# All block turns of the attention weights on VectorE, and one row-maximum instruction over two accumulators

## Time and profile before

| | us |
|---|---|
| median of 3 runs | 1153.29 (1152.88 to 1154.09) |
| the profiled execution, its own time | 1152.18 |
| its span, first to last instruction | 1150.4 |
| PE / DVE / ACT / POOL busy | 1120.2 / 904.9 / 588.6 / 658.0 |
| granted TensorE clock | 1.0 throughout |

### The profile page before, as it was taken

One profiled execution on the slowest core, in us unless ns is written; L12 is line 12 of the kernel. 1 busy time (PEld: TensorE's weight loads), 2 busy tenths in 40 slices (PEclk: granted clock), 3 DMA queues, 4 the chain that ended last, 5 costly groups with the idle time before them and its releaser, 6 DMA issues.

```text
span 1150.4 us, 19136 instructions
## 1 busy us (share of the span) xinstructions
PE 1120.2 (97%) x5885; PEld 856.2 (74%) x5885; DVE 904.9 (79%) x1656; ACT 588.6 (51%) x1332; POOL 658.0 (57%) x476
## 2 busy tenths in 40 slices
PE   7999999999999999999999999999999999999998
PEld 6888888888888888886666767767667666767655
DVE  7998787878787866578597797786887876976977
ACT  7634443434444344447455555555556545565543
POOL 2645252525252524329759579389398498496694
DMA  5441414141414132343324323324225233242241
GB/s 202 147 138 46 138 46 128 55 128 55 128 55 128 55 91 92 129 129 74 91 56 129 88 51 117 91 55 130 71 58 161 55 91 111 55 122 59 55 128 38
DMA packets 76606, 108.44 MB, mean 94 GB/s; under 512 B 7712, under 2 KB 40224, under 8 KB 76576
## 3 DMA queue, kind: packets, MB, share of 16 engines
q1 hardware_dynamic: 76576, 108.07, 31.0%
HBM read 58.76 MB, written 16.78 MB: 66 GB/s over the span
## 4 chain that ended last, share of the span: by engine, by line
PE 68%; POOL 13%; DVE 8%; issue 6%; ACT 4%; DVEq 0%; DMA 0%; POOLq 0%; ACTq 0%; SPq 0%
PE ps_f L992 23%; PE ps_s L992 8%; PE ps_o L2274 7%; PE ps_h L992 7%; POOL spare L1587 6%; PE ps_r L2200 6%; POOL spare L1593 5%; PE ps_r L2233 5%; PE ps_s L2251 4%; PE ps_r L2209 3%; DVE nmax L1860 3%; PE ps_s L2259 2%; DVE z_tmp L1879 2%; ACT probs_odd L1670 1%; POOL z L1605 1%
## 5 line engine op out<-in xcount | busy, mean ns | idle before, releaser
L1860 DVE TENSOR_REDUCE nmax<-ps_s 128x1 f32<-128x512 f32 x256 | 158.5, 680 | 79.0 <-PE ps_s L2251 78.0
L1587 POOL TENSOR_TENSOR spare<-xv,pick 128x512 f32<-128x512 f32 x160 | 184.8, 1155 | 35.0 <-DVE pick L1975 22.1
L1605 POOL TENSOR_TENSOR z<-z,z_tmp 128x1280 f32<-128x1280 f32 x35 | 102.6, 2932 | 138.6 <-DVE z_tmp L1879 136.3
L1593 POOL TENSOR_TENSOR spare<-spare 128x512 f32<-128x512 f32 x128 | 165.6, 1294 | 10.0
L1670 ACT ACTIVATE tmp<-ps_s,nmax 128x512 f32<-128x512 f32 x124 | 85.2, 687 | 97.1 <-DVE nmax L1860 97.1
L2274 PE MATMUL ps_o<-pt,spare 128*64 128x512 f32 x496 | 113.3, 598 | 6.6 <-POOL spare L1593 5.1
L254 POOL TENSOR_TENSOR e_t<-e_t 128x512 fp32r<-128x512 f32 x28 | 35.4, 1300 | 135.7 <-ACT e_t L510 135.7
L2251 PE MATMUL ps_s<-k,q 64*128 64x512 f32 x768 | 106.4, 408 | 3.1 <-ACT pt L1679 3.1
L2251 PEld LDWEIGHTS ps_s<-k,q 64*128 64x128 f32 x768 | 67.3, 184 | 49.3 <-issue 33.3
L254 POOL TENSOR_TENSOR c<-stage,c 128x512 fp32r<-128x512 f32 x28 | 42.3, 1542 | 94.4 <-ACT c L250 94.4
L2200 PE MATMUL ps_r<-es_t,c_t 128*128 128x512 f32 x384 | 96.3, 399 | 0.0
(11 more groups left out here) (245 smaller groups left out, 2272.2 us busy)
## 6 DMA issues: line engine op xcount, KB each, us to landing
pt<-tmp SPq DMA_DIRECT2D x248, 128.0 KB, 2.6
stage<-in_x SPq DMA_DIRECT2D x32, 256.0 KB, 3.2
x_sb<-in_x SPq DMA_DIRECT2D x8, 1024.0 KB, 5.3
x_dram<-x_sb SPq DMA_DIRECT2D x32, 256.0 KB, 3.1
stage<-x_dram SPq DMA_DIRECT2D x8, 1024.0 KB, 5.4
x_sb<-x_dram SPq DMA_DIRECT2D x8, 1024.0 KB, 5.4
out_dram<-x_sb SPq DMA_DIRECT2D x31, 256.0 KB, 2.6
stage<-in_ctx_t SPq DMA_DIRECT2D x28, 256.0 KB, 2.8
```

Source lines behind the costliest of these rows:

```text
L1587: pool.tensor_tensor(v_tmp[:] if e else acc, xv[:, :, e, :].unsqueeze(2).broadcast_to(shape), pick[:, e, :, 2 * p:2 * p + 2].unsqueeze(3). ...
L1593: pool.tensor_tensor(acc, acc, v_tmp[:], ALU.add).then_inc(v_steps, 1)
L1605: pool.tensor_tensor(zv, zv, z_tmp[:, h % 2], ALU.add).then_inc(z_pool, 1)
L1860: dve.tensor_reduce(nmax[:, n:n + 1], ps_s[:, n % BANKS, :], AX_X, ALU.max, negate=True).then_inc(nmax_ready, 1)
```

## The change

Odd tiles are no longer turned by PE and copied by ACT. ACT writes all four tiles of a round in blocks; DVE turns the two tiles of one head with one instruction of 128x1024, two a round, at the place AFTER and no longer TURNS; the four DMAs of a round carry 256 KB each and no longer 128 KB. PE's next scores wait for the exponentials alone. A row-maximum instruction covers the two banks of both heads' tiles (128x1024), two a round in place of four. The coefficients go from DVE to POOL, which now mixes them in between `mix_values` and the sums, in another order. The factors for `normalise` are copied by ACT. At round 11 `turn_z` is AFTER, and PE takes `values` 0 of the next batch ahead of it. The last two rounds keep PE's turns and ACT's copies, with the row maxima in pairs.

```diff
-            AT["turn_z", k] = (11, BEHIND)
+            AT["turn_z", k] = (11, AFTER)
...
 def move_blocks(b, r, first=False):
-                sp.wait_ge(blocks_turned, b * ODD_STEPS + (r + 1) * ODD_ROUND)
+                sp.wait_ge(blocks_turned, b * STEPS + (r + 1) * BANKS)
...
                 for q in range(QUADS):
-                    sp.dma_start(by_rows(2 * p % 4)[:, r % 2, q].rearrange("p k s a -> p (k s a)"),
-                                 probs_even[q * BLOCK:(q + 1) * BLOCK, r % 2].rearrange(
-                                     "p (j k) s a -> p j (k s a)", j=QUADS)).then_inc(moved[r % 2], 16)
+                    sp.dma_start(by_rows(p)[:, r % 2, q].rearrange("p k i s a -> p (k i s a)"),
+                                 probs[r % 2][q * BLOCK:(q + 1) * BLOCK].rearrange(
+                                     "p (j u) -> p j u", j=QUADS)).then_inc(moved[r % 2], 16)
...
+            def coefficients(b, p):
+                heads = slice(2 * p, 2 * p + 2)
+                pool.wait_ge(rden_ready, b * PAIRS + p + 1)
+                if p == 0:
+                    pool.wait_ge(mask_ready, b + 1)
+                pool.tensor_tensor(coef[:, heads], mask[:, :, :, heads].rearrange("p e t h -> p h t e"),
+                                   rden[:, heads, :].unsqueeze(3).broadcast_to([P, 2, NT, E]),
+                                   ALU.mult).then_inc(coef_ready, 1)
             def rest(b, first=False):
-                for p in range(1, PAIRS):
-                    mix_values(b, p, first)
-                for p in range(LAST_PAIR - 1):
-                    mix_sums(b, p)
+                mix_values(b, 1, first)
+                coefficients(b, 0)
+                mix_values(b, 2, first)
+                mix_sums(b, 0)
+                coefficients(b, 1)
+                mix_values(b, 3, first)
+                mix_sums(b, 1)
+                coefficients(b, 2)
...
             with pool.Fori(0, B - 2) as b:
+                coefficients(b, LAST_PAIR)
                 mix_sums(b, LAST_PAIR - 1)
                 mix_values(b + 1, 0)
                 rest(b + 1)
...
             def normalise(b, tiles):
+                if tiles[0] == 0:
+                    act.wait_ge(last_newton, ROOT_STEPS + 1)
+                    act.activation(norm[:], x1_norm[:, :, bass.ds(b * NT, NT)], ACT.Copy).then_inc(norm_ready, 1)
...
             def scores_exp(b, n, first):
                 act.wait_ge(nmax_ready, b * STEPS + n + 1)
...
+                if n % BANKS == 0 and (n >= 2 * BANKS or not first):
+                    act.wait_ge(moved[n // BANKS % 2], (b * PAIRS + n // PAIR) * MOVED)
+                act.activation(blocks(n), ps_s[:, n % BANKS, :].rearrange("p (j a) -> p j a", a=BLOCK), ACT.Exp,
+                               bias=nmax[:, n:n + 1], accum_out=den[:, h, t:t + 1]).then_inc(p_exp, 1)
-            def probs_copy(b, n, first):
...
             def row_max(b, n):
-                dve.wait_ge(s_ready, b * STEPS + n + 1)
-                dve.tensor_reduce(nmax[:, n:n + 1], ps_s[:, n % BANKS, :], AX_X, ALU.max, negate=True).then_inc(nmax_ready, 1)
+                dve.wait_ge(s_ready, b * STEPS + n + 2)
+                dve.tensor_reduce(nmax[:, n:n + 2], ps_s[:, n % BANKS:n % BANKS + 2, :], AX_X, ALU.max,
+                                  negate=True).then_inc(nmax_ready, 2)
-            def turn_blocks(b, n):
-                dve.wait_ge(p_exp, b * STEPS + n + 1)
-                dve.transpose(even_probs(n), even_probs(n)).then_inc(blocks_turned, 1)
+            def turn_blocks(b, r, i):
+                dve.wait_ge(p_exp, b * STEPS + r * BANKS + i + 3)
+                both_tiles = probs[r % 2].rearrange("p (j i u) -> p j i u", i=2, u=2 * BLOCK)[:, :, i, :]
+                dve.transpose(both_tiles, both_tiles).then_inc(blocks_turned, 2)
...
 @@ block.vector, step @@
                 elif place == TURNS:
-                    if 0 <= n < ROUNDS:
-                        for tile in range(n * BANKS, n * BANKS + BANKS, 2):
-                            turn_blocks(b, tile)
...
+                elif 0 <= n < ROUNDS:
+                    for i in range(2):
+                        turn_blocks(b, n, i)
...
 def scores(b, n, first, freed=None):
-                    pe.wait_ge(pt_ready, odd_turned(b, n + 1 - BANKS))
+                    pe.wait_ge(p_exp, b * STEPS + n + 2 - BANKS)
...
-                    elif place == TURNS:
-                        for tile in range(n * BANKS + 1, n * BANKS + BANKS, 2):
-                            turn_probs(b, tile)
...
-                    for place in PLACES:
+                    for place in PLACES[:AFTER]:
                         step(b, n, place)
                         step(b + 1, n - ROUNDS, place)
+                    step(b + 1, n - ROUNDS, AFTER)
+                    step(b, n, AFTER)
```

More of the change, by code:

```diff
@@ L87 @@
     spare: object
+    late: object
     tmp: object
@@ L1627, in _ @@
                 rest(b + 1)
+            coefficients(B - 2, LAST_PAIR)
             mix_sums(B - 2, LAST_PAIR - 1)
@@ L1630, in _ @@
                 mix_values(B - 1, p)
+                if p in (1, 2):
+                    coefficients(B - 1, p - 1)
             everything, second_tiles = slice(0, NT), HALVES[1][1]
             last_sum(3, everything, 0, 2)
-            pool.wait_ge(coef_ready, B * PAIRS)
+            pool.wait_ge(last_coef, 2)
             last_sum(4, everything, 1, 2)
@@ L1658, in scores_exp @@
                 h, t = head_tile(n)
-                scores = ps_s[:, n % BANKS, :]
-                if n % 2 == 0:
-                    if n >= 2 * BANKS or not first:
-                        act.wait_ge(moved[n // BANKS % 2], (b * PAIRS + n // PAIR) * MOVED)
-                    out, scores = even_probs(n), scores.rearrange("p (j a) -> p j a", a=BLOCK)
-                else:
-                    if n >= BANKS or not first:
-                        act.wait_ge(pt_ps, odd_turned(b, n - BANKS))
-                    out, scores = plainly(probs_odd[:, n % BANKS // 2, :]), scores_by_keys(scores)
-                act.activation(out, scores, ACT.Exp, bias=nmax[:, n:n + 1],
-                               accum_out=den[:, h, t:t + 1]).then_inc(p_exp, 1)
-            def probs_copy(b, n, first):
-                h, t = head_tile(n)
-                act.wait_ge(pt_ps, odd_turned(b, n))
-                if t == 0 and (h >= 4 or not first):
-                    act.wait_ge(o_ps, b * PAIRS + h // 2 - 1)
-                act.activation(turned(n), scored(n), ACT.Copy).then_inc(pt_ready, 1)
+                if n % BANKS == 0 and (n >= 2 * BANKS or not first):
+                    act.wait_ge(moved[n // BANKS % 2], (b * PAIRS + n // PAIR) * MOVED)
+                act.activation(blocks(n), ps_s[:, n % BANKS, :].rearrange("p (j a) -> p j a", a=BLOCK), ACT.Exp,
+                               bias=nmax[:, n:n + 1], accum_out=den[:, h, t:t + 1]).then_inc(p_exp, 1)
             def last_exp(b, n):
@@ L1767, in step @@
                         copy_last(b)
-                    if 0 <= n < ROUNDS:
-                        for tile in range(n * BANKS + 1, n * BANKS + BANKS, 2):
-                            probs_copy(b, tile, first)
                 elif place == BEHIND:
@@ L1985, in step @@
                 if place == SCORES:
-                    if n == NORMALISE_AT and not first:
-                        take_norm(b)
                     for p in range(PAIRS):
@@ L1991, in step @@
                     if 0 <= n < ROUNDS:
-                        for tile in range(n * BANKS, n * BANKS + BANKS):
+                        for tile in range(n * BANKS, n * BANKS + BANKS, 2):
                             row_max(b, tile)
@@ L2078, in last_rounds @@
                 row_sums(b, 2)
-                for n in tiles[:BANKS]:
+                for n in tiles[:BANKS:2]:
                     row_max(b, n)
-                coefficients(b, 2)
+                last_coefficients(b, 2)
                 for h in (2, 3):
@@ L2084, in last_rounds @@
                 last_add(2, everything, 3, 1)
-                for n in tiles[BANKS:]:
+                for n in tiles[BANKS::2]:
                     row_max(b, n)
@@ L2088, in last_rounds @@
                 row_sums(b, 3)
-                coefficients(b, 3)
+                last_coefficients(b, 3)
                 last_mix(5, turned_pair(2))
@@ L2272, in values @@
                     for a in range(2):
[L2273 removed]
+                        rows = by_rows(p)[:, :, :, k, a].rearrange("p r q s a -> p q r (s a)")
                         end = pe.matmul(ps_o[head_rows(a), :], v_acc[:, p, k, a, :], rows, start=k == 0,
```

67 lines of the change are left out of this document (25 added, 42 removed).

## The result

The changed kernel takes 1214.03 us (median of 4 runs, 1212.22 to 1214.84), the kernel before beside it 1153.09: 1.0526 times as long, 95% interval 1.0508 to 1.0544. The prediction was 1198 in a range of 1170 to 1212: slower, as forecast, but 16 us more, and 2 us above the range. The profiled execution took 1214.53.

What follows compares the result with a forecast made beforehand. PE looked like the bound (79.4 of 81.2 us), with DVE then POOL nearly as long. Six turns at +6.05 (36.3) plus 3.6, 3.3 and 3.1 made 46: 1152.2 + 46 = 1198 us, range 1170 to 1212 (own range 1185 to 1210).

Steps and rivals of the forecast that it cites:

- The main theory: Removed PE transposes become waiting for DVE and POOL, already as late as PE: +6.05 us a turn, 1198 us, chance 68%.
- four foretold waits: PE idle before round 10 for DVE's k (4.3 us), `values` 0 for POOL (5.3), `turn_y` (some 3), and experts 1.
- rival A: The removed PE work pays in full, 68.2 us off, giving 1084 us; chance 11% (12% in the numbers).
- rival B: DVE's lag does not cross from round 12 to rounds 5 and 6: a turn grows 1.5, 1171 us; chance 13%.
- Rival C: The 256 KB moves land late and exponentials wait for the buffer: 2 us a turn more, 1212 and above; 5%.
- (1): Round 8 to `values` 0: later logits put DVE's turns, 2.27 us, on the path behind q low; +2.6 us a turn.
- (2): `turn_z` behind `values` 0: it now stands between `values` 0 and round 12; +1.5 us a turn.
- (4): Round 5: DVE's turns of round 12 delay its maxima and with them the second y tile; +2.15 us a turn.
- (5): Round 6: round 5's delayed turns hold the maxima, and experts 1 waits for DVE behind them; +1.5 us a turn.
- Rival D: The merging of maxima does nothing, as back-to-back maxima hide nearly all fixed cost; already in the sum at 0.12 a round.
- The last batch: `values` 2 waits for round 5's DMAs, turned last, and starts 16.2 us into round 5: +3.1 us.
- The first batch: POOL's mixing ends at about 565 with a later pick, a sum and coefficients before pair 3; round 8 starts 3.6 later.

Runs made afterwards that it cites:

- the filled run: Changed kernel with PE's idle time ahead of round 10, `values` 0, `turn_y` and the last `values` 2 filled by transposes of the identity: 1206.87 us, 1.0447.
- SP's order: Changed kernel with the last batch's moves of round 5 issued ahead of SP's wait for the stored output: 1208.65 us; same edit in the kernel before: 1153.46 us.
- POOL's order: Changed kernel with `coefficients` 1 and `mix_values` 3 ahead of `mix_sums` 0 on POOL: 1213.7 us, 1.0529.

## Why the prediction was right or wrong, point by point

The main theory held: PE loses 68 us of work and gains none of it, since DVE and behind it POOL were already as late as PE in round 9. Of the four foretold waits each stands where it was put. Rival A (the PE work pays) and rival B (DVE's lag stays in round 12) are out: round 5 takes 14.64 us, not under 11. Rival C, the larger moves landing late in the steady turns, did not occur either: no `values` and no exponential in a steady turn waits for a DMA, though the moves take 4.5 us and not 2.6. (The chance of rival A stands as 11% with the rivals and 12% with the numbers; 12 is what makes the sum 100.)

By the steps, the stretches of one turn in the trace of after against the earlier trace rows, in us:

| | foretold | measured | of it clock |
|---|---|---|---|
| (1) round 8 to `values` 0 | +2.6 | +1.3 | 0 (1.5 hidden) |
| (2) `values` 0 to round 12 | +1.5 | +3.15 | 1.7 |
| (3) round 12 | -0.9 | -0.5 | |
| (4) round 5 | +2.15 | +3.7 | 1.5 |
| (5) round 6 | +1.5 | +0.7 | |
| (6) round 7 | -0.9 | -0.9 | |
| a turn | +6.05 | +7.5 | 3.2 |

- **Steps (2) and (4) failed in one way.** The places and the waits were right; the work behind the waits was priced at the durations of the earlier trace rows, all of them taken at full clock. Behind 2.2 and 3.2 us of idle PE ran it at the lower clock. That is 3.2 us by the rows; the filled run's turn at full clock gives back 2.6, 13.4 us over the six turns, and its longer wait at experts 1 is the other 0.6. It is no term of the sum at all, and most of the miss of 16 us; of the other errors, 7 us too much in the turns hide most of some 10 us too little at the ends, and that is luck.
- **Step (1) was too large.** Up to round 10 it is exact (19.6 us from round 8, 19.5 foretold). But POOL's chain from its first addition took 18.0 us (858.42 to 876.44), where the kernel before took 19.2 (the 19.4 of the prediction counts from the product's end): of its instructions one was stretched by 1.1 us where two had been, since, by the timelines, DVE's two-input additions now fall elsewhere (nothing was tried on that alone). So `values` 0 started 1.4 earlier than foretold. PE reached it 1.8 later, 1.5 of that with scores and transposes at the lower clock. Together these make the idle 2.2 us and not 5.3.
- **Step (5) was too large.** Round 5's turns end 0.14 us into round 6, and the maxima wait for the scores, not for the turns.
- **The merging.** The sum had its 0.5 us for the late first maximum once, at round 8, and called the rest 0.12 a round of gain. The run with four maxima gives 21 us, the merging in the kernel before -8.7. The delay counts wherever exponentials are waited for: rounds 8, 5 and 6, and where the clock falls behind it: 1.7 of the 3.1 us a turn is `values` 0 at full clock. Rival D, "the merging does nothing", was wrong with it, and so was the thought that fewer instructions could do no harm.
- **The place of the turns.** It was in steps (1) and (4) as 2.27 each, 4.5 a turn. The run that undoes it gives 36 us, 3.6 to 5.7 a turn in the timeline (30 in six) and the rest at the ends. But the split was wrong: rounds 8 and 9 take 18.8 us and not 19.6, round 5 11.2 and not 14.6, of which 1.5 is the clock. The place cost 0.75 where (1) had 2.27, and 1.9 where (4) had it; the rest came with the clock and in round 12 (9.1 and not 9.5).
- **The last batch failed by size.** Foretold +3.1, measured +9.4. DVE's turns ended at +11.0 into round 5, as worked out. But SP's queue, which the prediction put "at nothing", was not free: the wait for stored output held the moves 3.4 us, four issues took 4.2 us and not 2.5, and they landed later, at 4.6 and not 2.6. The run with SP's order gives back 5.
- **The first batch** was +5.2 at round 8, not 3.6; 1.3 of that is in the first stage already, which the change does not touch; in the profiled execution with SP's order, where this stretch is the same code, round 8 is at +4.0. POOL's order is worth nothing in the medians. It was not followed further.

Together: six turns 42.8 us (foretold 36.3), the first batch 5.2 (3.6), the last turn's rounds 4.0 (3.3), the last batch 9.4 (3.1), the end 1.0 (0): unrounded 62.3, the difference of the spans. The estimate of 1.22 us by the formula of the Trainium skill (VectorE: DVE Perf Modes, "The TRN2 errata") agrees with the 1.205 and 1.219 us that the lines view gives for one 1024-element instruction, but is not the pitch of 1.12 and 1.15 between two back to back. The Trainium skill (VectorE: DVE Perf Modes, "The DRAIN you can't avoid") says that the next instruction starts only when the pipe is empty, but adds what the prediction passed over: a next one that is not held starts earlier. The pitches here agree with that exception; where instructions follow one another, the pitch is the price.

With place and maxima undone 15.4 us over the kernel before remain; the two that undo SP's order as well and reorder DVE's round 9, one with POOL's product moved too, are 8.9 and 9.9 over it. The rows put the rest on POOL: on the path from DVE's products through POOL to `values` 0, which stays some 18 us long whatever PE saves, on that from there to the logits, and on the last moves; how much the moves of twice the size cost by themselves was not tried.

## What to carry to other kernels

Before taking work off the busiest engine, lay the others' last results beside its starts: where they arrive as late as it does, the work removed turns into waiting, and on TensorE the waiting can make what comes next slower too, so an idle time of 2 us and more ahead of a matmul group had to be priced twice here, unless another wait stood behind it. An instruction that merges two waits makes the first consumer wait for the second producer; here it saved DVE 0.15 us a round (2.24 for four tiles where it was 2.39), and made everybody who waited for the first half wait 0.5 longer. When two engines tie, look for a piece of the shorter-looking chain that can start earlier: one 1.05 us product moved into POOL's idle time was worth more here than 68 us of transposes taken from PE.

## What the runs showed of the hardware that was not expected

- The same sixteen matmuls took 3.65 us at a granted clock of 1.00 and 5.35 behind an idle time of about 2.2 us, with the clock at 0.68 in the mean; in these runs they kept 3.65 behind 0.6 to 1.7 us of idle, did either behind 2.1 to 2.4, and took 5.1 to 6.6 behind 3.3 us and more. In the changed kernel, behind 4.27 us twelve score matmuls took 2.93 for 1.66, at a clock of 0.50.
- A DVE instruction on 128x160 elements with two inputs in SBUF took 2.89 and 2.51 us for 0.33 when it was started while POOL was in a long addition, and ended within 0.2 us of POOL's end; ahead of that addition it took 0.33 again. The Trainium skill (SBUF — State Buffer, "SBUF: two separate sides") has the rule for it: VectorE and GpSimd share one pair of ports, the one that starts first holds it for its whole instruction, and a VectorE instruction with two SBUF inputs is locked out meanwhile; both runs agree, with 2.89 and 0.33. The other way round, a 512-element POOL instruction takes 1.1 us more where a two-input DVE addition falls on it (2.42 for 1.29, at 869.03 in the changed kernel, beside DVE's addition from 868.35 to 870.30).
- Four issues of 128 KB moves took SP 2.5 us, four of 256 KB in the changed kernel 3.6 to 4.2, and the median to landing went from 2.6 to 4.5 us.
